# Opening products in column groups, and cross attention's first chunk placed before the end of self attention

## What is computed

```
# layer 0, on x [4, 1024, 512] and a context [4, 64, 512], 16 heads of 32
x = x + selfattn(ln(x)) @ W1 + b1       # causal; scores q.k * sqrt(32), softmax, values
x = x + crossattn(ln(x), ctx) @ W2 + b2 # keys and values from the context
x = x + relu(ln(x) @ Wf1 + bf1) @ Wf2 + bf2
# layer 1, a gated fusion of x with one vector per batch made from the context
vp   = mean(ctx, 1) @ Wv.T + bv                        # one row per batch
tp   = x @ Wt.T + bt
rw   = softmax over the 1024 rows of 2 * sum(tp * vp)  # the last round of three
gate = sigmoid(tp @ Wg_t.T + (rw * vp) @ Wg_v.T + bg)
out  = layernorm(x + gate * rw * vp)
```

## Time and profile before

| | |
|---|---|
| median of 3 runs | 2246.68 us (2243.13 to 2246.86) |
| the profiled execution | 2245.24 us, its span 2243.3 us |
| granted TensorE clock, mean | 0.983 |
| busy share PE, PEld, DVE, ACT, POOL | 96%, 73%, 68%, 46%, 41% |
| opening, to the first attention scores | 0 to 110 us |
| self attention | 110 to 971 us |
| first cross score | 995.4 us |
| moved by transfers | 295.00 MB, mean 132 GB/s |

### The profile page before, as it was taken

How to read it: one execution, slowest core, us unless ns; L and a number is a source line. 1 busy time by engine, 2 the same in 40 slices (tenths; PEclk the granted TensorE clock), 3 DMA queues, 4 the chain that set the end, 5 groups by cost and what they waited for, 6 DMA issues and landing times. The chain is left out here.

```text
span 2243.3 us, 35511 instructions
## 1 busy us (share of the span) xinstructions
PE 2144.4 (96%) x12742; PEld 1641.4 (73%) x12742; DVE 1526.4 (68%) x3714; ACT 1025.1 (46%) x1905; POOL 912.5 (41%) x954
## 2 busy tenths in 40 slices
PE   7999999999999999989999998999999999999997
PEld 5666666666666664557777777788888888888885
DVE  5577766776786667456666668674667758675857
ACT  4155655665565556533433445452433334243423
POOL 1067777777777778563333333220110101010102
PEclk9999999999999998899999999999999999999998
DMA  7655555565555555211111131685566556656531
GB/s 235 78 82 99 95 81 84 104 97 82 87 106 84 88 81 141 73 66 57 57 57 62 57 118 71 227 319 186 182 222 216 211 194 224 223 214 216 195 138 52
DMA packets 115556, 295.00 MB, mean 132 GB/s; under 512 B 19358, under 2 KB 24478, under 8 KB 107184
## 3 DMA queue, kind: packets, MB, share of 16 engines
q1 hardware_dynamic: 115380, 292.74, 47.9%
HBM read 186.43 MB, written 54.81 MB: 108 GB/s over the span
## 5 line engine op out<-in xcount | busy, mean ns | idle before, releaser
L740 POOL TENSOR_TENSOR es<-es,er 128x512 f32<-128x512 f32 (+3 forms) x640 | 587.9, 959 | 258.7 <-PE psum L880 244.1
L981 ACT ACTIVATE er<-psum 128x512 f32<-128x512 f32 (+3 forms) x640 | 278.5, 471 | 287.0 <-DVE psum L1097 175.0
L1086 DVE CUSTOM_DVE_ANT_0 psum<-psum,mask_ts 128x384 f32<-128x384 f32 (+3 forms) x512 | 249.1, 502 | 154.2 <-PE psum L825 151.8
L825 PE MATMUL psum<-ks,qs 96*128 96x512 f32 (+3 forms) x768 | 260.6, 371 | 5.8 <-DVE mx L1086 2.7
L868 PE MATMUL psum<-qs,ks 100*128 100x512 f32 (+3 forms) x768 | 251.6, 364 | 12.0 <-DVE mx L1086 6.3
L55 PE MATMUL psum<-fah,fb 128*128 128x256 f32 x896 | 254.5, 284 | 0.0
L57 PE MATMUL psum<-fah,fb 128*128 128x256 f32 x896 | 253.5, 283 | 0.0
L56 PE MATMUL psum<-fal,fb 128*128 128x256 f32 x896 | 253.3, 283 | 0.0
L2084 ACT ACTIVATE hh<-psum,cols 128x512 fp32r<-128x512 f32 x128 | 88.1, 688 | 305.8 <-DVE psum L2169 305.5
L825 PEld LDWEIGHTS psum<-ks,qs 96*128 96x128 f32 x768 | 139.7, 191 | 115.2 <-issue 33.3
L1090 DVE TENSOR_REDUCE mx<-psum 128x1 fp32r<-128x512 f32 x256 | 175.4, 685 | 60.2 <-PE psum L825 59.4
(11 more groups left out here) (286 smaller groups left out, 4926.3 us busy)
## 6 DMA issues: line engine op xcount, KB each, us to landing
fb<-w_d SPq DMA_DIRECT2D x56, 1792.0 KB, 7.5
qs<-stage SPq DMA_DIRECT2D x96, 256.0 KB, 5.7
ks<-stage SPq DMA_DIRECT2D x96, 256.0 KB, 8.2
w_d<-fb SPq DMA_DIRECT2D x8, 1792.0 KB, 6.8
rs<-rs_d SPq DMA_DIRECT2D x32, 256.0 KB
sa_d<-rs SPq DMA_DIRECT2D x32, 256.0 KB, 2.1
sx<-sa_d SPq DMA_DIRECT2D x8, 1024.0 KB, 5.9
xt<-in_x SPq DMA_DIRECT2D x32, 256.0 KB, 6.2
```

The source lines that it names most:

```text
L740: e.tensor_tensor(es, es, er, ALU.add).then_inc(s_add.sem, 1)
L825: t = e.matmul(bank1(*s)[:, v * wd:v * wd + wd], Q.qs[par][0:96, i, 128 * ti:128 * ti + 128], Q.ks[par][0:96, i, c0:c0 + wd], start=True, ...
L981: e.activation(dst, bank1("sc", g, c2, j, i)[:, off:512], ACT.Exp, scale=SCALE).then_inc(s_freeS.sem, 1)
L1086: t = e.tensor_tensor_reduce(out=ps, in0=ps, in1=mask_ts[:, 512 - wd:512], scale=1.0, scalar=-3e38, op0=ALU.add, op1=ALU.max, accum_out=mx ...
```

## The change

Five edits of the opening:

- The bias fold `wb` becomes three steps: `wq` multiplies each slice of the weight with a 128x32 block whose first column is the slice of `be1` and whose rest is zero, each slice into its own column group of 32 partitions, as a product of its own; `wc` copies the bank to memory (ACT); `wb` adds the partial products over the partitions, with 4 products with a column of ones.
- Units 4 to 8 become `q` (partial products of the means with Wv in four column groups), 8 and 4 (the rows and the columns, each from the copied partial products with a 128x32 matrix `pick` that adds what belongs together).
- Units 9, 10 and 12 become one unit 9: three products in three column groups, accumulated over four slices in turn.
- `Z.pad` holds the padded columns; a memset, two copies and a reduction on DVE make them and `pick` at the start. `early_done` waits for the last bias fold as well.
- The due times of the opening are new: the first two units `z` stand between the first transposes, the bias folds are later, and the row maxima of group 0 end after its first scores (`MAX_0`).

And in the preparation of cross attention:

- Buffers: the raw weights, `wkv`, `ct` and `bvc` get places that are free from the end of the projections on, chunk 0's queries and the first four tiles' `pp` get places of their own. `2kc`, `2kb` and `2ldc` of chunk 0 wait for `projected` alone.
- Banks: the bias fold, keys, values and all of chunk 0 take banks from `banks1`. The values come before the keys, with their own semaphore.
- Due times: chunk 0's load and W1 product are placed in groups 14 and 15, its turn and its first two query products in the second half of group 15, the other two after it; the first tile moves from 16.793 to 16.448.
- The feed-forward's `nm` of chunk 0 moves from ACT to DVE, and one turn of each later chunk from -0.313 to -0.12 of its plan.

```diff
-PROJ_0 = (27.2, 31.3, 37.9, 40.4)
+PROJ_0 = (27.2, 31.3, 37.9, 42.338)
...
-VALUES_0 = (40.2, 52.3, 66.7, 68.9)
+VALUES_0 = (40.2, 48.438, 66.7, 73.343)
...
-MAX_0 = -0.007
+MAX_0 = 0.073
...
+OPEN_LOAD = (1.33, 1.6, 1.7, 1.8, 24.5)
+OPEN_SPLIT = (18.0, 23.818, 32.0)
+OPEN_ROWS = 3.681
+OPEN_TURN = 11.0
+OPEN_Z = (11.0, 14.5, 22.07, 21.5, 31.471, 38.142, 39.0, 50.183, 52.0)
+OPEN_FOLD = (18.663, 24.262, 61.166)
+OPEN_FOLDED = (0.653, 3.959)
...
+    for j, at in enumerate(OPEN_FOLD):
+        t += [(at0(at + a), (s, j)) for a, s in ((0, "wq"), (OPEN_FOLDED[0], "wc"), (OPEN_FOLDED[1], "wb"))]
+    for u, at in zip((0, 1, 2, 3, "q", 8, 4, 11, 9), OPEN_Z):
+        t += [(at0(at), ("z", u)), (at0(at + (2.5 if u in (0, 1, 2, 3) else 1.5)), ("ze", u))]
...
+    first = {("2w1", 1, 0, 0): 0, ("2w1", 1, 1, 0): 1, ("2w1", 1, 2, 0): 2, ("2s", 0, 0): 3, ("2s", 0, 2): 4, ("2tu", 0, 0): 5, ("2tu", 0, 1): 6}
+    until = {first[s]: at for at, s in order if s in first}
...
-CROSS_AT = 16.793
-CROSS_LOAD = (14.019, 14.431, 14.754, 14.309, 15.318)
-CROSS_SPLIT = (14.581, 14.853, 15.576)
-CROSS_ONCE = (14.168, 15.027, 14.983, 15.099, 14.261, 15.089, 15.146, 14.946)
-CROSS_KEYS = (15.173, 15.19, 15.199, 15.461, 15.405)
-CROSS_0 = (15.723, 15.776, 15.812, 16.19)
+FIN_LAST = 0.2
+CROSS_AT = 16.448
+CROSS_LOAD = (14.019, 14.56, 15.659, 14.1, 15.114)
+CROSS_SPLIT = (14.56, 14.9, 15.9)
+CROSS_ONCE = (14.565, 14.2, 14.754, 14.88, 14.603, 15.089, 15.146, 14.601)
+CROSS_KEYS = (15.35, 15.37, 15.366, 14.95, 14.97)
+CROSS_0 = (14.18, 14.75, 14.85, 0.09, 15.25, (15.4, 0.03), (15.6, 15.7, 16.05, 16.08), (15.7, 15.8, 16.12, 16.15))
...
+                Z.orow = sb(early, "orow", [NB, C])
+                Z.rows = sb(early, "zrows", [128, C])
+                Z.bg = sb(early, "bgrow", [128, C])
+                Z.part = sb(early, "zpart", [128, C])
+                Z.fold = sb(early, "wbpart", [128, C])
+                Z.pad = sb(early, "zpad", [128, 4, KT, 32])
+                Z.pick = sb(early, "zpick", [128, 32])
+                Z.ocb = sb(early, "ocb", [NB, 1])
...
-            w.wait_ge(s_mm0, 13)
+            w.wait_ge(s_mm0, 9)
+            w.wait_ge(s_bmm, 6)
...
+                    if u == "q":
+                        for k in range(KT):
+                            t = e.matmul(ps[32 * k:32 * k + 32, :], pl[:, k, :], Z.wv[:, k, :], start=True, stop=True)
+                    elif u == 8:
+                        t = e.matmul(ps[0:NB, :], Z.pick[:, 0:NB], Z.part[:], start=True, stop=True)
+                    elif u == 4:
+                        for m in range(4):
+                            t = e.matmul(ps[:, 4 * m:4 * m + 4], Z.part[:, 128 * m:128 * m + 128], Z.pick[:, 0:NB], start=True, stop=True)
+                    elif u == 11:
+                        for k in range(KT):
+                            t = e.matmul(ps[0:NB, 0:1], vcol[:, k, 0:NB], bt[:, k:k + 1], start=k == 0, stop=k == 3)
+                    elif u == 9:
+                        for k in range(KT):
+                            for n, (lhs, rhs) in enumerate(((vcol, Z.wt[:, k, :]), (vcol, Z.wg[:, 4 + k, :]), (btp, Z.wg[:, k, :]))):
+                                t = e.matmul(ps[32 * n:32 * n + 32, :], lhs[:, k, :], rhs, start=k == 0, stop=k == 3)
...
+                elif s[0] == "wq":
+                    j = s[1]
+                    w.wait_ge(d_raw1[j % 2], 16 * (j // 2 + 1))
+                    w.wait_ge(s_ones, 5)
+                    w.wait_ge(s_bw, 2 * j)
+                    free1(w, *s)
                     for k in range(KT):
...
+                        t = e.matmul(bank1(*s)[32 * k:32 * k + 32, :], bep[:, k, :], raw1(j)[:, k, :], start=True, stop=True)
+                    t.then_inc(s_bmm.sem, 1)
...
+                    for m in range(4):
+                        t = e.matmul(bank1(*s)[:, m:m + 1], Z.fold[:, 128 * m:128 * m + 128], ones[:, 0:1], start=True, stop=True)
+                    t.then_inc(s_bmm.sem, 1)
...
+            e.memset(Z.pad[:], 0.0).then_inc(s_ones.sem, 1)
             w.wait_ge(d_cols, 16)
+            w.wait_ge(s_ones, 3)
+            e.tensor_copy(btp[:, :, 0:1], bt.unsqueeze(2)).then_inc(s_ones.sem, 1)
+            e.tensor_copy(bep[:, :, 0:1], cols[:, col_at["be1"]:col_at["be1"] + 4].unsqueeze(2)).then_inc(s_ones.sem, 1)
+            e.tensor_reduce(Z.pick[:], ident[:].rearrange("p (k n) -> p n k", k=4), AX, ALU.add).then_inc(s_ones.sem, 1)
...
-            R.W = {nm: (sb(ctx, f"{nm}h", [128, KT, C], F32R), sb(ctx, f"{nm}l", [128, KT, C], F32R))
-                   for nm in ("W1", "Wq_c", "W2")}
-            R.qh, R.ql = [sb(ctx, "qh0", [128, 4, 512], F32R)], [sb(ctx, "ql0", [128, 4, 512], F32R)]
             with ExitStack() as early:
-                R.raw = [sb(early, f"raw2{j}", [128, KT, C]) for j in range(2)]
+                sb(early, "pairs1q", [128, 4, KT, C])
                 R.wkv = sb(early, "wkv", [128, KT, C])
                 R.ct = sb(early, "ctc", [128, KT, 256])
                 bvc = sb(early, "bvc", [128, C])
+            R.W, R.raw = {}, []
+            for nm in ("W1", "Wq_c", "W2"):
+                hi = sb(ctx, f"{nm}h", [128, KT, C], F32R)
+                with ExitStack() as early:
+                    R.raw.append(sb(early, f"raw{nm}", [128, KT, C]))
+                R.W[nm] = hi, sb(ctx, f"{nm}l", [128, KT, C], F32R)
+            with ExitStack() as early:
+                first_q = [sb(early, "q0b", [128, 2, 2, 512], F32R)]
+                first_pp = [sb(early, f"pp0{p}", [128, 16, S]) for p in range(2)]
+            R.qh, R.ql = [sb(ctx, "qh0", [128, 4, 512], F32R)], [sb(ctx, "ql0", [128, 4, 512], F32R)]
             R.ah, R.al = sb(ctx, "ah", [128, KT, 512], F32R), sb(ctx, "al", [128, KT, 512], F32R)
             R.sx = sb(ctx, "sx", [128, 4, C])
             R.xt = [sb(ctx, "xt0", [128, 4, C])]
             R.qh.append(sb(ctx, "qh1", [128, 4, 512], F32R))
             R.ql.append(sb(ctx, "ql1", [128, 4, 512], F32R))
             R.vb = sb(ctx, "vb", [128, NB, C])
+            with ExitStack() as early:
+                first_q.insert(0, sb(early, "q0a", [128, 2, 2, 512], F32R))
...
+            return bank[R.useI[s[:3]] % 3] if s[1] else bank1(*s[:3])
+
+        def query(c, m):
+
+            return tuple(first_q[m // 2][:, n, m % 2, :] if c == 0 else (R.qh, R.ql)[n][c % 2][:, m, :] for n in range(2))
+
+        def pp(n):
+
+            return first_pp[n % 2] if n < 4 else R.pp[n % 2]
+
...
+        def freeI(w, s):
+
+            u = R.useI[s[:3]]
+            if u < 12:
+                free1(w, *s[:3])
+            elif u < 15:
+                over1(w, u - 12)
...
                     filledI(w, ("2cT", c - 1, 3))
                 else:
-                    w.wait_ge(s_vb, 8)
+                    projected(w)
                 w.wait_ge(d_sa, 16 * (2 * (4 * (c // 2) + 3) + c % 2 + 1))
...
                     w.wait_ge(s_fillP, 4 * (c - 2) + 4)
+                    if c == 2:
+                        filledT(w, ("2tu", 3, 1))
+                elif c == 0 and m < 2:
+                    w.wait_ge(s_fillV, 4)
                 else:
                     attended(w)
...
+            elif s[0] == "nm" and s[1] == 0:
+                i, sm = s[2], small[:, 0, :]
+                w.wait_ge(s_rs3, 2)
+                filledI(w, ("2cT", 7, 3))
+                e.tensor_scalar(rows3(0)[:, i, :], F.xt[0][:, i, :], sm[:, 64 + 2 * i:65 + 2 * i], sm[:, 104 + i:105 + i],
+                                ALU.subtract, ALU.mult).then_inc(s_nm3.sem, 1)
...
```

283 lines of the change are left out of this document (138 added, 145 removed).

## The result

The changed kernel takes **2228.86 us** (median of 4 runs, 2227.93 to 2229.62) beside 2245.16 us before (4 runs, 2243.13 to 2246.86): ratio 0.9926, 95% interval 0.9913 to 0.9938. Some 16.4 us came off where I had forecast 36.4. The direction was right and the size less than half. The end also took 6 us for the transition where its own bounds said 8 to 26; with 8 it would have been 2227. The profiled execution took 2229.62 us, span 2227.5, so the two traces differ by 15.8 us.

The account below looks back on a forecast made before the run. TensorE, busy 96% of the span, was taken as the bound. The opening's 18.0 us and the transition's 18.4 took 36.4 off 2245.24, giving 2208.8, or 2210 against the three-run median; range 2198 to 2229.

Parts of the forecast that it names:

- The end: Upper end, 2229 us, of the range: 2246.7 less 12 for the opening and 6 for the transition.
- The opening's sum: Opening: cheaper TensorE products and an earlier fill together gain 18.0 us (12 to 22).
- I take 0 for them: Opening: SP's output rows and later prefetch of the next head group's halves cost 0, 2 us as bad end.
- 98% busy TensorE has no slack to absorb a shift: After the opening: its gain of 18 us remains at every later mark.
- shift-absorbed rival: A later wait that both kernels share absorbs the shift, leaving 2246 us; chance 0.02.
- DVE at the maxima: Rival, opening: DVE bounds the bursts of maxima, half the opening's gain stays, 2219 us; chance 0.10.
- The transition's tail: Last attention product to first cross score: 24.4 us falls to 8.0, gaining 16.4.
- The transition's body: 883 to 971 us: waits gone 8.6 to 12, adds come 6 to 11; net 2 us gained, bounds 8 lost, 10 gained.
- Beyond the body's price: Transition: SP's chunk 0 issues (about 3 us) precede the sums' transfers, needed only later; inside the body's bounds.
- POOL and DVE hold the transition: Rival: moved splits and adds in POOL's fullest stretch leave the tail only 5 us net, 2224 us; chance 0.14.
- keeps its work, 0: Feed-forward: the moved turn in the later chunks was priced at 0.
- the price from the trace's row: Opening: four column groups take 1.06 us together; units 9, 10 and 12's three rows priced at 3.7 us.

Follow-up runs that it names:

- e5: Changed kernel with head group 1's fourth stacking step (three 256 KB transfers) issued behind the second small copy of maxima; 2224.98 us.
- e7: e6 with e5's edit, the late stacking step, added; no faster than e5 alone.
- e12: e10 with e5's edit, the late stacking step, added; ratio 0.9900 to the kernel before.
- e13: e12 with the query weights' loads issued from 14.45 and their fold at 14.9; nothing gained.
- e14: e12 with two pairs of output transfers at 49 us of the plan instead of 26; median 3 us better, overlapping intervals.
- e1: The opening's part of the change alone, against the kernel before; 0.38% faster, some 8.6 us.
- e2: The other part alone (cross stage, last sums, feed-forward), opening as before, against the kernel before; 2238.99 us, 0.23% faster.
- e17: e12 with the edits of e13 and e14 and the eight context copies on ACT instead of DVE; 2212.85 us, ratio 0.9860.
- e8: Changed kernel with the four normalisations of the feed-forward's first chunk back on ACT; median 3.5 us higher.
- e3: Changed kernel with the eight context copies on DVE 0.3 head groups later, behind the first weight's splits; not faster.
- e6: Changed kernel with the transition's loads, biases, weights, fold and context copies reordered at both places at once; did not gain.
- e10: e6 with chunk 0's splits taking their minuend from PSUM, written there by ACT; ratio 0.9920, 7.6 us faster than e6.

## Why the direction was right and the size wrong

**The opening's sum was right, its arrival was not.** The new blocks cost 3.6, 3.2, 2.8, 1.1, 1.0 and 0.9 us, as priced; unit 9's three rows run side by side, from 64.45 to 68.08, 3.6 us. The first weight product started at 14.80 instead of 19.36 us (forecast 14.7). With its one late stacking step mended the lead at the sums of head group 2 is 18.2 to 19.3 us (e5, e7, e12, e13), where I had 18.0. The step that failed is "I take 0 for them", for the queues: SP's prefetch of the next head group's halves. I had noted that it is needed only later, and not asked what it would be ahead of: the order put its last step in front of the small copy that the first group's second chunk waits for. That cost 3.7 us and the clock behind it. The other wait, 2.2 us before the first maxima, stayed in e14. The first attention scores came at 90.68, forecast 88.

**"98% busy TensorE has no slack to absorb a shift", and the shift-absorbed rival at 0.02, were wrong by 4 us.** Between the sums of head groups 13 and 14 the lead falls from 13.8 to 9.8 in the changed kernel and from 13.0 to 9.9 in e1; the first 2 to 3 us of it lie where the sums' transfers make POOL late. I had written that only a wait on something not ordered by the engines could do that, and that I saw none; the softmax sums go through four transfers a chunk and are exactly that. In e2, without the shift, nothing is lost by the second chunk of head group 13 and 1.5 us by the sums of group 14 (849.2). How much goes differs, 1.4 us in e17 and 5 in e5, and no run shows what sets it.

**DVE at the maxima** did not become the bound: 6.6 of 9.5 us busy in the first stretch, 10.7 of 14.5 in the next. That rival is out.

**The transition's tail was right**: 9.6 us for 8.0 forecast and 24.4 before; in e17 8.3.

**The transition's body is the step that failed**, at "Beyond the body's price, SP's issues for chunk 0 (about 3 us) move ahead of the softmax sums' small transfers; each of those is used only a third of a head group later", and at what the list left out. Net 2 us gained was forecast, with 8 lost as the bad end; 15 lost was measured. I had counted SP's issue time, not what some 4.5 MB of loads (1 MB each of the attention output, x and Wv, three quarters of W1, and the broadcast biases) do to a write of 8 KB that SP, DVE and TensorE wait for in turn: 9.8 us from the write to the read behind it, 3.8 before. And the eight copies (`2cd`) were not in my sum, a moved step of DVE, put beside POOL's adds. I had counted POOL's adds that move, four splits and nothing else. The trace of before had the warning:

```profile
L1488 DVE COPY pp<-ctc x8: 278/278/2743, 896.1 to 900.0; 128x256 f32<-128x256 f32 x8
```

The first copy took 2.74 us, to 898.8, where a row of POOL's adds ends (898.67); the seven behind it, with POOL all but idle, took 0.28.

With both mended (e17) the body is 109.8 us, against 107.0 before and some 105 by my forecast. TensorE waits 8.4 us in it, 3.1 of them for exponentials; whether POOL's pace sets these I did not try.

**The rival "POOL and DVE hold the transition"** had the mechanism, at a chance of 0.14, and 2224 was nearer than my 2210. That the total came so near is luck, since its 18 us for the opening and its 5 for the transition both failed and the 6 us after the first cross score were not in it. It was mis-sized too: I priced a split beside POOL at 1.56 us, one instruction's worth of waiting. It can be a whole row of POOL's work, 13.59 us. The Trainium skill, SBUF — State Buffer, section SBUF: two separate sides, says that a DVE instruction with two SBUF inputs and a GpSimd one that reads SBUF exclude each other for a whole instruction. By that rule the trace agrees on who excludes whom: two SBUF inputs 13.59 us, one in PSUM 0.69. The copies, which have one SBUF input, were held too (9.72 us), and the rule for two inputs does not cover them. The Trainium skill gives the side that "starts first" the pair "for the whole instruction"; the runs show that through some ten adds in a row DVE may not come in between at all.

**After the first cross score** the lead grew by 6.2 us, forecast 0. Besides the 1 to 2 us of the normalisations, two parts are visible. Before, TensorE waits 3.3 us in seven places of the feed-forward for DVE's rows, in e1 too, and not in the changed kernel, e2 or e8:

```profile
PE psum L1962 <- DVE fx L2204: 3.3, 7, 0.9
```

```profile
PE psum L2002 <- DVE fx L2244: 3.3, 7, 0.9
```

The first row is of the kernel before, the second of e1. e2 and e8 share with the changed kernel, and not with e1, the moved turn of the seven later chunks, for which I wrote "keeps its work, 0". It is the likely cause, worth about 3 us; but it was not run alone, and the other edits of that half are not excluded. The other part, 2.9 us, is the last products, which ran at half clock in the one trace of before and at full in that of after, behind the same wait of 1.8 us; I read that as chance of an execution, and no run decides it.

**Column groups side by side.** By the Trainium skill, TensorE: Matmul & The Clock Gate, Measured speedup vs the span model, the three rows would take 4.4 us (an estimate); they took 3.6, so the price from the trace's row was the right one. Of the drain of which the Trainium skill, TensorEngine Tiling (Array Packing), Tiling Modes, speaks nothing shows beside blocks of 1.06 us.

**Not tried:** the transition mended in its transfers with the copies left on DVE but POOL's adds moved; the moved turn alone; a shorter chain for the sums.

## What to carry to other kernels

When a step is moved, list for each of its instructions, the DMAs too, who else stands in the same queue and which other engine's instructions run beside it at the new place; work that cost nothing at an idle time can cost a row of another engine's instructions at a busy one. Before moving a DVE instruction with SBUF operands alone beside a GpSimd stream, put one operand into PSUM or give the copy to ACT. And when two late things run side by side, mending one can show nothing: follow the next wait in the trace before giving the cause up.

## What the runs showed of the hardware

- A DVE split with both inputs in SBUF took 0.74 us alone, and 10.01 (e3) and 13.59 us (e6) when it got no turn until POOL's row of adds ended; with one input in PSUM it took 0.69 beside the same adds (e10). A DVE copy within SBUF took 0.28 us alone, 1.35 with one turn between two adds (changed kernel) and 9.72 with none (e13). ACT's copies beside such a row: 0.40 us (e17).
- Stacking transfers, 256 KB each from SBUF to SBUF, fill all 16 DMA engines at 127 GB/s (share 1.09, changed kernel, 56 to 65.5 us), where the stretch with the loads from memory in it moves 386 GB/s at a share of 1.05 (before, 10 to 20 us). A copy of 24 KB behind them was there 10.7 us after its issue.
- An 8 KB write issued into full DMA engines held the read that waits for it back by 9.8 us (changed kernel, 851.60 to 861.38), 3.8 before (862.13 to 865.89).
